# Four transformer layers on one core: the first two batches' keys and values of a 16-head attention are projected in the layer before its own, and VectorE's order in the third layer changes

## The chip, the cores and the metric

The kernel runs on one core of a Trainium2 chip. A core has five engines that run their own instruction streams and meet through semaphores: TensorE (PE in the rows), VectorE (DVE), ScalarE (ACT), GpSimd (POOL) and SyncE (SP), which here only issues DMA transfers. PEld is TensorE's loading of weights, which goes on beside its matrix multiplications. The metric is the device time of one launch in microseconds (us); lower is better.

## The reference

Activations `x` of 8 batches x 256 tokens x 256 features pass four layers, all in float32. Each layer is an attention block and then a feed-forward block, each with a normalization of its input and a residual sum.

- Layer 0: 4-head attention over a context with rotary positions and a mask; then 8 experts (256 to 512 to 256), the best two of each token.
- Layer 1: attention with 16 heads of 16 features. Queries come from the normalized `x`; **keys and values are `ctx @ Wk + bk` and `ctx @ Wv + bv`**, that is, from the context alone, which no layer changes. Then 8 experts again, of which each token takes two.
- Layer 2: an mLSTM block (4 heads, a decay matrix made from gates) and a squared-ReLU block that mixes each token with the one before it.
- Layer 3: attention as in layer 1 with weights of its own; then 8 gated experts with a capacity.

Since the keys and values of layers 1 and 3 depend on `ctx` and weights alone, they can be computed at any time before their attention.

## The kernel before, in words

Each layer with experts is one block of five engine programs: `in_one_block` (line 87) runs on every engine first the attention's program and then the experts'. Between blocks stands a barrier. The order within an engine is the order in which the Python code issues; there is no scheduler. SBUF tensors of a layer are its own, among them `took`, a 1 MB workspace that the attention and the experts share, and `mha_vaug`, which holds the values of two batches beside a column of ones. The weights of all layers (`kept_w_mha` and others) are loaded once at the start.

**16-head attention** (`mha_block`, layers 1 and 3). Batches go through in 64 steps `u` of two heads, eight steps per batch. A step computes scores on TensorE (L560), VectorE reduces each row's extreme (L417, `maximum`), TensorE turns these (L580), VectorE adds them into the queries (L427, `top`), and three steps later TensorE computes the scores again, transposed (L568), ScalarE takes the exponential (L310), and L595 multiplies by the values. `scores(u)` waits for the maxima of step u-1. The next batch is prepared in between, at fixed steps: `turn_x` at step 0, `project_q` at 1, `project_k` at 2 (ScalarE's `keys`, L288, takes it out of PSUM), `project_v` at 4 (VectorE's `values`, L406, at 5). For batch 0 all of it stands in front of the loop. In layer 1 the order there is keys, values, `turn_x` (L499), queries; in layer 3 it is `turn_x`, keys, queries, values. `keep_busy` issues dummy multiplications of a constant (L150). The context of a batch comes by a SyncE DMA into `mha_ctxT` (L233), two slots. At its start ScalarE fills `mha_vaug` with ones (L280).

**Experts** (`moe_block`). Their programs begin with what is left of routing for the last two batches: on TensorE `count(B-2)`, 6 dummy matmuls, `turn(B-1)` (L805), `route(B-1)` (L828), 2 dummies, `count(B-1)`, 6 dummies, a wait for the tile bounds, 18 dummies and then the first tile. VectorE normalizes the last batch (L795), lays out padding rows (`lay_pads`, L1183 to L1192), chooses the experts of the last batch (`choose`, L837 on) and places its tokens; GpSimd then scatters the rows to HBM (L910), and SyncE loads the first tile when all are scattered.

**Third layer** (`l2`). A loop of turns `w_` from 0 to 8: a turn has the mLSTM of batch `w_` and, one turn behind, the feed-forward block of batch `w_-1`. VectorE's part of a turn began with `f_mean_and_var(w_-1)` (L2098 to L2103, on `l_f_stats`), which waits for GpSimd's residual sum (L1967). Then came `weigh` of heads 0 and 1 (L2204: scores in PSUM times the decays that ScalarE made, L2024), `gate_rows` (L2164), `f_normalize` (L2157) and the rest. On TensorE `spread` makes the decays' exponents; `turn_z` (L2373) waits for `gate_rows`, the second `qk` for `weigh` of heads 0 and 1, and `turn_f` (L2350 on `l_fxn`) for `f_normalize`, in this order.

## Time and profile before

| | us |
|---|---|
| median of 3 runs | 1388.36 (1384.16 to 1397.91) |
| profiled execution | 1390.65 |
| its span, first to last instruction | 1388.9 |

| engine | busy us | share of the span |
|---|---|---|
| TensorE | 1263.5 | 91% |
| VectorE | 849.8 | 61% |
| ScalarE | 479.6 | 35% |
| GpSimd | 446.7 | 32% |

The blocks lie on the span as follows: layer 0 from 0 to 322 (its experts from 156), layer 1 from 322 to about 765 (experts from 556), layer 2 to 952, layer 3 to the end. The granted clock of TensorE, mean over the span, is 0.967 of full. In a timeline row stand the start in us, the length, the engine, the line of the code, the operation, what it writes and reads, its count, and in brackets the idle time before it and what ended that.

### The profile page before, as it was taken

What the parts mean: (1) busy time and instruction counts of PE and PEld (TensorE: products, weight loads), DVE (VectorE), ACT (ScalarE), POOL (GpSimd) and SP (SyncE); (2) the same over time, 40 slices, a digit from 0 to 9 for tenths busy, and PEclk for the clock granted to TensorE, in tenths of its full rate; (3) what the DMA queues carried; (4) which work ended last, traced back from release to release, by engine and by line L of the source; (5) the groups of instructions that cost most, each with busy time, mean ns of one, the idle gap of its engine ahead of it and who ended that gap; (6) DMA issues with size and microseconds to landing.
All of it is one profiled execution on the core that took longest, in us unless ns stands there. A gap on an engine that the chain in (4) does not pass through costs nothing. (4 is left out here: it accounts for less than half of the span.)

```text
span 1388.9 us, 31670 instructions
## 1 busy us (share of the span) xinstructions
PE 1263.5 (91%) x9966; PEld 1016.5 (73%) x9966; DVE 849.8 (61%) x2819; ACT 479.6 (35%) x1123; POOL 446.7 (32%) x421
## 2 busy tenths in 40 slices
PE   5899899997899998899999899998899998899995
PEld 4676689995566665799887777876566665799995
DVE  6788444445577876544465588564567776465663
ACT  3655211113456554011111244343556554111110
POOL 1245612222134333522122255432134343222231
PEclk9999899999999999999999998799999999999998
DMA  9201234422101401464654100000001011645523
GB/s 309 71 17 40 93 99 141 134 69 80 46 25 40 165 33 38 138 210 155 200 176 145 51 16 1 1 1 24 8 17 48 33 40 54 212 103 145 146 46 87
DMA packets 87557, 120.08 MB, mean 86 GB/s; under 512 B 11248, under 2 KB 64752, under 8 KB 87152
## 3 DMA queue, kind: packets, MB, share of 16 engines
q1 hardware_dynamic: 48656, 55.20, 12.9%
q10 hardware_dynamic: 25632, 34.85, 7.7%
q0 software_dynamic: 13152, 28.54, 7.3%
q8 instruction: 64, 1.05, 0.3%
q14 instruction: 53, 0.43, 0.1%
HBM read 82.53 MB, written 38.13 MB: 87 GB/s over the span
## 5 line engine op out<-in xcount | busy, mean ns | idle before, releaser
L1351 PEld LDWEIGHTS bank<-f_xT,f_up 128*128 128x128 f32 x2144 | 253.5, 192 | 14.9 <-issue 7.9
L1351 PE MATMUL bank<-f_xT,f_up 128*128 128x128 f32 x2144 | 258.7, 276 | 3.1 <-DVE f_xT L1227 2.1
L417 DVE TENSOR_REDUCE mha_nmax<-bank 128x2 f32<-128x512 f32 x256 | 170.1, 686 | 119.1 <-PE bank L560 95.4
L1360 PE MATMUL bank<-f_down,f_hT 128*128 128x256 f32 x832 | 199.5, 381 | 4.0 <-DVE f_hT L1268 2.8
L310 ACT ACTIVATE l_took<-bank 128x512 f32<-128x512 f32 x256 | 138.9, 598 | 130.8 <-PE bank L568 130.8
L560 PE MATMUL bank<-l_took,mha_q 32*128 32x256 f32 x1024 | 147.7, 406 | 33.2 <-DVE mha_nmax L417 21.8
L1360 PEld LDWEIGHTS bank<-f_down,f_hT 128*128 128x128 f32 x832 | 149.2, 190 | 24.0 <-DVE f_hT L1268 5.6
L1116 POOL DMA_INDIRECT yout<-f_y,f_to x66 | 81.0, 1228 | 244.2 <-DVE f_y L1304 107.6
L568 PE MATMUL bank<-l_took 32*128 32x256 f32 x1024 | 145.5, 406 | 0.7 <-ACT l_took L310 0.7
L560 PEld LDWEIGHTS bank<-l_took,mha_q 32*128 32x128 f32 x1024 | 90.5, 186 | 73.6 <-DVE mha_nmax L417 44.9
L1167 ACT ACTIVATE f_hT<-bank,f_b 128x128 f32<-128x128 f32 x148 | 46.2, 363 | 276.4 <-PE bank L1351 276.4
L150 PE MATMUL bank<-consts 128*128 128x256 f32 x430 | 109.9, 412 | 11.3 <-PEq L69 8.6
L910 POOL DMA_INDIRECT rows<-r_src,r_slots x96 | 95.1, 990 | 59.2 <-DVE r_slots L903 35.1
L150 PEld LDWEIGHTS bank<-consts 128*128 128x128 f32 x430 | 86.5, 207 | 26.2 <-issue 13.6
L1268 DVE TENSOR_SCALAR f_hT<-bank,f_b 128x128 f32<-128x128 f32 x148 | 45.1, 346 | 78.2 <-PE bank L1351 76.4
L568 PEld LDWEIGHTS bank<-l_took 32*128 32x128 f32 x1024 | 87.5, 186 | 2.2 <-issue 2.2
L1162 ACT ACTIVATE f_gate<-bank 128x256 f32<-128x256 f32 x60 | 22.5, 383 | 153.8 <-PE bank L1351 153.8
L260 POOL TENSOR_TENSOR mha_rstd<-mha_var_eps,consts 128x2 f32<-128x2 f32 x16 | 11.6, 726 | 192.9 <-DVE mha_var_eps L386 192.8
L595 PE MATMUL bank<-l_took,mha_vaug 128*32 128x256 f32 x1024 | 70.0, 392 | 1.8 <-ACT l_took L310 1.8
L790 POOL TENSOR_TENSOR r_rstd<-r_var_eps,consts 128x2 f32<-128x2 f32 x24 | 17.7, 737 | 144.3 <-DVE r_var_eps L784 144.3
L595 PEld LDWEIGHTS bank<-l_took,mha_vaug 128*32 128x32 f32 x1024 | 27.1, 110 | 34.8 <-issue 22.1
L1237 DVE COPY f_xt<-l_took 128x256 f32 (+1 forms) x91 | 28.1, 308 | 35.1 <-DMA l_took<-rows 35.0
(290 smaller groups left out, 2278.7 us busy)
## 6 DMA issues: line engine op xcount, KB each, us to landing
l_took<-rows SPq DMA_DIRECT2D x91, 132.0 KB, 2.1
f_up<-in_W ACTq DMA_DIRECT2D x23, 512.0 KB, 4.5
f_down<-in_W ACTq DMA_DIRECT2D x18, 512.0 KB, 5.5
l_took<-rows SPq DMA_DIRECT2D x21, 264.0 KB, 2.8
f_up<-in_W SPq DMA_DIRECT2D x9, 512.0 KB, 7.3
ring<-yout SPq DMA_DIRECT2D x8, 512.0 KB, 4.0
mha_ctxT<-in_ctxT SPq DMA_DIRECT2D x16, 256.0 KB, 2.9
f_down<-in_W SPq DMA_DIRECT2D x6, 512.0 KB, 9.1
```

Of the source, the lines that this page charges most:

```text
L150: pe.matmul(bank[:, 0:S], G.const("ident"), G.consts[:, 0:S], start=True, stop=True)
L310: act.activation(probT[:, n % SLOTS, :, :].rearrange("p c s -> p (c s)"), transposed_in(n)[:, :], ACT.Exp, scale=-1.0).then_inc(prob_ready, 1)
L417: vector.tensor_reduce(nmax[:, p, :, at], ps_s[n % 2][:, :].rearrange("p (k s) -> p k s", s=S), AX.X, ALU.min).then_inc(max_ready, 1)
L560: ins = pe.matmul(ps_s[j][:, part * S:(part + 1) * S], q[row:row + 32, r, p, c, at], k[row:row + 32, r, p, c, :], start=True, stop=True)
L568: ins = pe.matmul(transposed_in(2 * t + j)[:, part * S:(part + 1) * S], k[row:row + 32, r, p, c, at], q_top[row:row + 32, r, p, c, :], sta ...
L595: ins = pe.matmul(values_in(g)[32 * j:32 * j + VW, 0:S], vaug[:, b % 2, c, 4 * i + j, :], probT[:, (4 * g + j) % SLOTS, c, :], start=c == ...
L910: pool.indirect_dma_start(rows[:, :], bass.IndirectOffsetOnAxis(self.slots[:, t, k:k + 1], 0), self.src[:, t, :], None).then_inc(self.scat ...
L1116: pool.indirect_dma_start(away[:, :], bass.IndirectOffsetOnAxis(to[:, k:k + 1], 0), (z if p else y)[:, k, 0:width], None, compute_op=ALU.a ...
L1167: ins = act.activation(hT[:, m, :], ps_h[0][:, m * R:(m + 1) * R], ACT.Relu, bias=b1[:, e, m:m + 1])
L1268: ins = vector.tensor_scalar(hT[:, m, :], ps_h[1][:, (m - 2) * R:(m - 1) * R], b1[:, e, m:m + 1], 0.0, ALU.add, ALU.max)
L1351: ins = pe.matmul(into, up[q][i][:, c, m * P:(m + 1) * P], xT[:, c, :], start=c == 0, stop=c == DC - 1)
L1360: ins = pe.matmul(ps_y[:, 0:D], hT[:, m, :], down[q][:, m, :], start=m == 0, stop=m == HC - 1)
```

## The change

1. A new class `Ahead` projects keys and values of batches 0 and 1 of a 16-head attention in the layer before: those of layer 1 at the start of layer 0's experts, those of layer 3 at the start of layer 1's experts (layer 2 then lies in between and leaves them alone). `took` and `vaug` become tensors of the whole program, so that the results stay.
2. Its context comes by two SyncE DMAs of 256 KB that wait for the last values of the attention (`pv_done`), since they land in its workspace. They stand in SyncE's queue behind the first expert weights and biases, and ahead of the wait for `ends_ready`.
3. Each batch takes 8 matmuls of 128x256 on TensorE, 4 activations on ScalarE and 2 additions on VectorE. The matmuls take the place of the two groups of 6 dummies; the 18 dummies in front of the first tile become 16 in layers 0 and 1; layer 3, which has 24, keeps all of its dummies. TensorE waits for the readers of the new results ahead of the first tile.
4. In `mha_block` nothing of keys and values is left for batches 0 and 1, and the contexts of batches 2 and 3 are loaded at its start. The ones are written once, by GpSimd at the very start of the program.
5. In the third layer VectorE does `weigh` of heads 0 and 1 ahead of `f_mean_and_var`, and `log_forget` ahead of `z_mean_and_var`.

```diff
+            if filled:
+                pool.memset(G.vaug[:, :, :, :, :], 1.0).then_inc(filled, 1)
             attend.gpsimd(pool)
...
+AHEAD = 2
...
+class Ahead:
...
+        self.ctxT = took[:, 6:6 + AHEAD, :, :]
+        self.k = took[:, 12:16, :, :].rearrange("p (r i) c s -> p r i c s", i=2)
+        self.keys_in, self.values_in = (G.PS[6], G.PS[0]), (G.PS[5], G.PS[2])
...
+    def load(self, eng):
+        eng.wait_ge(self.read, self.count)
+        for b in range(AHEAD):
+            eng.dma_start(self.ctxT[:, b, :, :], self.ctx_t[b].rearrange("(c p) n -> p c n", p=P)).then_inc(self.ctx_landed, 16)
+    def project(self, pe, b):
+        if b == 0:
+            pe.wait_ge(self.w_landed, 16 * 2)
+            pe.wait_ge(self.ctx_landed, 16 * AHEAD)
+        for m in range(DC):
+            for c in range(DC):
+                ins = pe.matmul(self.keys_in[b][:, m * S:(m + 1) * S], self.w[:, 1, c, m * P:(m + 1) * P], self.ctxT[:, b, c, :],
+                                start=c == 0, stop=c == DC - 1)
+        ins.then_inc(self.k_done, 1)
+        for i in range(TPB):
+            for c in range(DC):
+                ins = pe.matmul(self.values_in[b][:, i * D:(i + 1) * D], self.ctxT[:, b, c, i * P:(i + 1) * P], self.w[:, 2, c, :],
+                                start=c == 0, stop=c == DC - 1)
+        ins.then_inc(self.v_done, 1)
+    def keys(self, act, b):
+        bk = self.vec[:, 2 * DC:4 * DC]
+        if b == 0:
+            act.wait_ge(self.w_landed, 16 * 2)
+        act.wait_ge(self.k_done, b + 1)
+        for p, rows in enumerate(("even16", "odd16")):
+            for c in range(DC):
+                ins = act.activation(self.k[:, b, p, c, :], self.keys_in[b][:, c * S:(c + 1) * S], ACT.Identity,
+                                     bias=bk[:, DC * p + c:DC * p + c + 1], scale=self.G.const(rows))
+        ins.then_inc(self.k_ready, 1)
+    def values(self, vector, b):
+        bv = self.vec[:, 4 * DC:4 * DC + D]
+        if b == 0:
+            vector.wait_ge(self.w_landed, 16 * 2)
+            if self.filled:
+                vector.wait_ge(self.filled, 1)
+        vector.wait_ge(self.v_done, b + 1)
+        for i in range(TPB):
+            ins = vector.tensor_tensor(self.G.vaug[:, b, i, :, 0:D // MHA_HEADS],
+                                       self.values_in[b][:, i * D:(i + 1) * D].rearrange("p (h v) -> p h v", h=MHA_HEADS),
+                                       bv.rearrange("p (h v) -> p h v", h=MHA_HEADS), ALU.add)
+        ins.then_inc(self.v_ready, 1)
+    def all_read(self, eng):
+        eng.wait_ge(self.k_ready, AHEAD)
+        eng.wait_ge(self.v_ready, AHEAD)
...
-    vaug = sb("vaug", [P, 2, TPB, HEADS, VW])
+    vaug = G.vaug
...
-            after(sync, v_done, b - 1)
-            sync.dma_start(ctxT[:, b % 2, :, :], ctx_t[b].rearrange("(c p) n -> p c n", p=P)).then_inc(ctx_landed[b % 2], 16)
+            if b >= AHEAD:
+                after(sync, v_done, b - 1 - AHEAD)
+                sync.dma_start(ctxT[:, b % 2, :, :], ctx_t[b].rearrange("(c p) n -> p c n", p=P)).then_inc(ctx_landed[b % 2], 16)
...
-        act.activation(vaug[:, :, :, :, :].rearrange("p r i h v -> p (r i h v)"), first(2 * TPB * HEADS * VW), ACT.Identity,
-                       bias=1.0, scale=0.0).then_inc(ones_ready, 1)
         def keys(b):
-            act.wait_ge(k_done, b + 1)
+            if b < AHEAD:
+                act.sem_inc(k_ready, 1)
+                return
+            act.wait_ge(k_done, b + 1 - AHEAD)
...
-            vector.wait_ge(v_done, b + 1)
+            if b < AHEAD:
+                vector.sem_inc(v_ready, 1)
+                return
+            vector.wait_ge(v_done, b + 1 - AHEAD)
...
-            pe.wait_ge(ctx_landed[b % 2], 16 * (b // 2 + 1))
-            after(pe, xnT_ready, b + 1 if b else 0)
-            project(1, ctxT[:, b % 2, :, :], ps_x if b else ps_s[0]).then_inc(k_done, 1)
+            pe.wait_ge(ctx_landed[b % 2], 16 * (b // 2 + 1 - AHEAD // 2))
+            pe.wait_ge(xnT_ready, b + 1)
+            project(1, ctxT[:, b % 2, :, :], ps_x).then_inc(k_done, 1)
...
-        if incoming:
-            project_k(0)
-            project_v(0)
-            turn_x(0)
-            project_q(0)
-        else:
-            turn_x(0)
-            project_k(0)
-            project_q(0)
-            project_v(0)
+        turn_x(0)
+        project_q(0)
...
-            if s == 2 and b + 1 < B:
+            if s == 2 and AHEAD <= b + 1 < B:
...
-            if s == 4 and b + 1 < B:
+            if s == 4 and AHEAD <= b + 1 < B:
...
+        if ahead:
+            ahead.load(sync)
         sync.wait_ge(rt.ends_ready, 1)
...
         rt.turned(act, B - 1)
+        if ahead:
+            ahead.keys(act, 0)
         if BOOST or SUMMED:
             rt.weigh(act, B - 1)
         act.wait_ge(rt.ends_ready, 1)
         rt.pad(act, 0, pads[0], (1,))
+        if ahead:
+            ahead.keys(act, 1)
...
         lay_pads()
+        if ahead:
+            ahead.values(vector, 0)
         rt.choose(vector, B - 1)
         rt.place(vector, B - 1)
         rt.bound(vector)
+        if ahead:
+            ahead.values(vector, 1)
...
         rt.count(pe, B - 2)
-        keep_busy(pe, G, PS[7], 6)
+        if ahead:
+            ahead.project(pe, 0)
+        else:
+            keep_busy(pe, G, PS[7], 6)
         rt.turn(pe, B - 1)
         rt.route(pe, B - 1)
         keep_busy(pe, G, PS[7], 2)
         rt.count(pe, B - 1)
-        keep_busy(pe, G, PS[7], 6)
+        if ahead:
+            ahead.project(pe, 1)
+        else:
+            keep_busy(pe, G, PS[7], 6)
         pe.wait_ge(rt.bounds_ready, 1)
         for p, at in enumerate(passes):
             prime(pe, at.xT_done, at.h_done, at.y_done)
             ends = [end_of(pe, p, 0)]
-            keep_busy(pe, G, PS[7], 28 if p else 24 if GLU else 18)
+            keep_busy(pe, G, PS[7], 28 if p else 24 if GLU else 16)
+            if ahead and p == 0:
+                ahead.all_read(pe)
...
+        sems, took = semaphores(nc, ctx, "l0_"), G.took
         rt = Dispatch(nc, G, ctx, sems, "r0_", "route0", True)
         attend = l0_attention(nc, G, ctx, sems, took, a, rt)
-        experts = moe_block(nc, G, ctx, sems, took, "f0_", rt, (a["W1_0"], a["W2_0"]), (a["b1_0"], a["b2_0"]), leaving=handed)
-        in_one_block(nc, G.PS, rt, attend, experts)
+        ahead = Ahead(G, sems, took, "mha1", a["ctxT"], attend.read, attend.count, sems("vaug_filled"))
+        experts = moe_block(nc, G, ctx, sems, took, "f0_", rt, (a["W1_0"], a["W2_0"]), (a["b1_0"], a["b2_0"]), leaving=handed,
+                            ahead=ahead)
+        in_one_block(nc, G, rt, attend, experts, ahead.filled)
...
+        ahead = Ahead(G, sems, took, "mha3", a["ctxT"], attend.read, attend.count)
...
                 now, more = w_ < B, w_ + 1 < B
-                if w_ >= LAG:
-                    f_mean_and_var(w_ - LAG)
                 if now:
                     weigh(w_, 0)
                     weigh(w_, 1)
+                if w_ >= LAG:
+                    f_mean_and_var(w_ - LAG)
...
+                if more:
+                    log_forget(w_ + 1)
                 if w_ + 3 < B:
                     z_mean_and_var(w_ + 3)
-                if more:
-                    log_forget(w_ + 1)
...
+        took = ctx.enter_context(nc.sbuf_tensor("took", [P, NT, 2, D], F32))
+        vaug = ctx.enter_context(nc.sbuf_tensor("vaug", [P, AHEAD, TPB, MHA_HEADS, MHA_VW], F32))
```

TensorE, start of layer 0's experts, in the kernel before:

```order
L875 MATMUL bank<-r_chosen,r_ones 128x8
L150 MATMUL bank<-consts 128x256 x6
L805 MATMUL bank<-consts,r_src 128x128 x4
L828 MATMUL bank<-kept_w_route,r_xT 128x8 x4
L150 MATMUL bank<-consts 128x256 x2
```

and now:

```order
L941 MATMUL bank<-r_chosen,r_ones 128x8
L193 MATMUL bank<-took,kept_w_mha 128x256 x4
L198 MATMUL bank<-kept_w_mha,took 128x256 x4
L871 MATMUL bank<-consts,r_src 128x128 x4
L894 MATMUL bank<-kept_w_route,r_xT 128x8 x4
L155 MATMUL bank<-consts 128x256 x2
```

Where six dummies stood, the key projection (L193) and the value projection (L198) of batch 0 stand, ahead of the turn of the last batch (L805, now L871).

TensorE, start of layer 1's attention, before:

```order
L150 MATMUL bank<-consts 128x256 x5
L506 MATMUL bank<-mha_ctxT,kept_w_mha 128x256 x4
L534 MATMUL bank<-kept_w_mha,mha_ctxT 128x256 x4
L499 MATMUL bank<-consts,mha_xn 128x128 x4
L506 MATMUL bank<-mha_xnT,kept_w_mha 128x256 x4
L560 MATMUL bank<-l_took,mha_q 128x256 x4
L499 MATMUL bank<-consts,mha_xn 128x128 x4
L560 MATMUL bank<-l_took,mha_q 128x256 x4
L506 MATMUL bank<-mha_xnT,kept_w_mha 128x256 x4
```

and now:

```order
L155 MATMUL bank<-consts 128x256 x5
L575 MATMUL bank<-consts,mha_xn 128x128 x4
L582 MATMUL bank<-mha_xnT,kept_w_mha 128x256 x4
L634 MATMUL bank<-took,mha_q 128x256 x4
L575 MATMUL bank<-consts,mha_xn 128x128 x4
L634 MATMUL bank<-took,mha_q 128x256 x4
L582 MATMUL bank<-mha_xnT,kept_w_mha 128x256 x4
```

The key and value projections of batch 0 (L506 and L534 on `mha_ctxT`) are gone; `turn_x` and the queries follow the dummies.

VectorE, a turn of the third layer, before:

```order
L2121 SCALAR_TENSOR_TENSOR X<-l_fused,l_z_rstd,X 128x256 x2
L2098 BN_STATS l_f_stats<-X 128x6 x2
L2101 BN_AGGR l_f_moments<-l_f_stats 128x2 x2
L2103 TENSOR_SCALAR l_f_var_eps<-l_f_moments 128x2
L2204 SCALAR_TENSOR_TENSOR l_cT<-bank,l_decay 128x384 x2
L2164 TENSOR_SCALAR l_z_rows<-bank,kept_gate_bias 8x256
L2157 TENSOR_SCALAR l_fxn<-X,l_f_moments,l_f_rstd 128x256 x2
```

and now:

```order
L2201 SCALAR_TENSOR_TENSOR X<-l_fused,l_z_rstd,X 128x256 x2
L2284 SCALAR_TENSOR_TENSOR l_cT<-bank,l_decay 128x384 x2
L2178 BN_STATS l_f_stats<-X 128x6 x2
L2181 BN_AGGR l_f_moments<-l_f_stats 128x2 x2
L2183 TENSOR_SCALAR l_f_var_eps<-l_f_moments 128x2
L2244 TENSOR_SCALAR l_z_rows<-bank,kept_gate_bias 8x256
L2237 TENSOR_SCALAR l_fxn<-X,l_f_moments,l_f_rstd 128x256 x2
```

`weigh` of two heads (L2204, now L2284) has moved from behind the feed-forward block's moments to ahead of them; `gate_rows` (now L2244) follows the moments.

## Rows read from the trace of the kernel before

**Rows 1.** The page: busy time by engine; two DMA issues (KB each, us to landing)

```profile
PE 1263.5 (91%) x9966; PEld 1016.5 (73%) x9966; DVE 849.8 (61%) x2819; ACT 479.6 (35%) x1123; POOL 446.7 (32%) x421
...
mha_ctxT<-in_ctxT SPq DMA_DIRECT2D x16, 256.0 KB, 2.9
...
f_down<-in_W SPq DMA_DIRECT2D x6, 512.0 KB, 9.1
```

**Rows 2.** Timeline (start, us, engine, line), layer 1's first heads

```profile
332.58 0.76 DVE L406 TENSOR_TENSOR mha_vaug<-bank,kept_v_mha 128x256 f32<-128x256 f32 x2
...
333.25 0.99 DVE L448 TENSOR_SCALAR mha_q<-bank,mha_q_scale,mha_nbq 128x256 f32<-128x256 f32 x2
...
334.34 1.13 PE L560 MATMUL bank<-l_took,mha_q 32*128 32x256 f32 x8 [1.72 <-ACT mha_q L303]
...
335.95 0.66 PE L499 MATMUL bank<-consts,mha_xn 128*128 128x128 f32 x4 [0.48 <-POOL mha_xn L246]
```

**Rows 3.** Timeline, layer 1, values of batch 1

```profile
350.04 2.60 PE L534 MATMUL bank<-kept_w_mha,mha_ctxT 128*128 128x256 f32 x8
...
350.62 0.68 DVE L417 TENSOR_REDUCE mha_nmax<-bank 128x2 f32<-128x512 f32 x1
...
352.57 0.48 PE L560 MATMUL bank<-l_took,mha_q 32*128 32x256 f32 x2
```

**Rows 4.** Timeline, fourth layer's attention, its start

```profile
956.77 1.89 PE L506 MATMUL bank<-mha_ctxT,kept_w_mha 128*128 128x256 f32 x8
...
962.05 1.13 PE L560 MATMUL bank<-l_took,mha_q 32*128 32x256 f32 x8
...
965.62 3.58 PE L506 MATMUL bank<-mha_xnT,kept_w_mha 128*128 128x256 f32 x8
...
972.45 1.93 ACT L288 ACTIVATE l_took<-bank,kept_v_mha,consts 128x256 f32<-128x256 f32 x4 [1.28 <-PE bank L506]
```

**Rows 5.** Timeline, from layer 0's attention to its experts, TensorE

```profile
148.29 1.08 PE L1781 MATMUL bank<-l_took,a_v 128*64 128x256 f32 x8
...
156.31 4.52 PE L150 MATMUL bank<-consts 128*128 128x256 f32 x12
...
161.96 0.66 PE L805 MATMUL bank<-consts,r_src 128*128 128x128 f32 x4 [1.13 <-DVE r_src L795]
```

**Rows 6.** Timeline, layer 1's experts, routing of the last batch

```profile
562.58 0.18 DVE L837 TENSOR_TENSOR r_logits<-bank,kept_b_route 128x16 f32<-128x16 f32 x1 [0.19 <-PE bank L828]
```

**Rows 7.** Timeline, third layer, VectorE's first turn, then one later turn

```profile
778.41 0.87 DVE L2121 SCALAR_TENSOR_TENSOR X<-l_fused,l_z_rstd,X 128x256 f32<-128x256 f32 x2
...
836.86 1.89 DVE L2121 SCALAR_TENSOR_TENSOR X<-l_fused,l_z_rstd,X 128x256 f32<-128x256 f32 x2
...
837.54 1.35 ACT L2024 ACTIVATE l_decay<-bank,l_g 128x256 f32<-128x256 f32 x4 [1.18 <-PE bank L2409]
...
838.54 1.33 POOL L1967 TENSOR_TENSOR X<-X,l_h 128x512 f32<-128x512 f32 x1
...
839.91 0.75 DVE L2098 BATCH_NORM_STATS2 l_f_stats<-X 128x6 f32<-128x256 f32 x2 [1.16 <-POOL X L1967]
...
841.10 1.02 DVE L2204 SCALAR_TENSOR_TENSOR l_cT<-bank,l_decay 128x384 f32<-128x384 f32 x2
...
841.23 0.71 POOL L1954 TENSOR_TENSOR l_f_rstd<-l_f_var_eps,consts 128x2 f32<-128x2 f32 x1
...
842.43 0.71 DVE L2157 TENSOR_SCALAR l_fxn<-X,l_f_moments,l_f_rstd 128x256 f32<-128x256 f32 x2
...
842.55 0.29 PE L2373 MATMUL bank<-consts,l_z_rows 8*128 8x8 f32 x2 [0.89 <-DVE l_z_rows L2164]
...
844.18 1.11 PE L2350 MATMUL bank<-consts,l_fxn 128*128 128x128 f32 x4
```

**Rows 8.** Windows, third layer, TensorE: length, busy (count), granted clock, DMA share, GB/s

```profile
863.00:879.00 16.00, 16.00 (x66) 0.57 0.01 2
...
887.00:899.00 12.00, 12.00 (x56) 0.57 0.01 2
```

49 lines of the change are left out of this document (27 added, 22 removed).

## The prediction

> **What bounds the kernel now.** I read the page first, then a timeline of each place that the change touches, then windows for TensorE's clock. The page shows TensorE busy for 1263.5 us of the span [rows 1]: what stands in its queue is nearly always on the path, but only where it is not waiting for someone. So I ask at each place what TensorE waits for. In a 16-head attention the loop is a round trip of TensorE and VectorE: scores, maxima, scores. A projection put between two steps is free as long as it fits beside VectorE's maxima, and costs only the rest. Where the routing of the last batch runs, in front of the experts, TensorE waits for VectorE and dummies fill its time. In the third layer the path runs through VectorE and GpSimd and back to TensorE, and TensorE stands idle in front of L2373 [rows 7].
>
> The sum is made against the profiled execution, 1390.65 us, which is 2.3 above the median of 1388.36. What a measurement tells from no change is about 1%, 13.9 us: 1374.5 and 1402.2 are the bounds.
>
> **Part 1: keys and values leave the start of the attention.**
>
> *Layer 1, batch 0.* The first scores start at 334.34 [rows 2]. In front of them VectorE adds the values from 332.58 for 0.76 and scales the queries from 333.25 for 0.99. Without the additions the queries come 0.67 earlier, and so would the first scores, to 333.7. But `turn_x` of batch 1 stands next on TensorE and waits for GpSimd's `mha_xn` until 335.95, which the change does not touch [rows 2]; only the scores behind it can profit. I take 0.2, between 0 and 0.7.
>
> *Layer 1, batch 1.* Of its keys, the 4 activations (1.93 by the row of layer 3 [rows 4]) stood ahead of the first exponentials, which step 4 waits for; without them I take 0.4. Of its values, TensorE's projection takes 2.60 from 350.04, and the next scores start at 352.57, while VectorE's last maximum is done at 350.62 + 0.68 = 351.30 [rows 3]. A handover from VectorE to TensorE takes at least 0.1 (334.24 to 334.34 [rows 2]); the scores could start at 351.4 or some tenths later: 0.9. The key projection in step 2 lay beside VectorE's maxima: 0. Layer 1 in all: **-1.5**.
>
> *Layer 3, batch 0.* Here the keys (1.89 from 956.77) stand between `turn_x` and the queries, which need only ScalarE's copy of the turned input; that copy can run beside the keys, so between 0 and 1.89 of them is uncovered, and I take half, 0.9. The first scores (962.05) and all behind come 0.9 earlier [rows 4]. Batch 1 as in layer 1: 0.3 for the exponentials behind 1.93 us of ScalarE at 972.45, 1.0 for the values. Layer 3: **-2.2**.
>
> The bounds of both together: 0 if something else is late each time; and 16 us if all the TensorE time counted, four projections per layer at 1.89 [rows 4] to 2.60 [rows 3]. I stay near the low end, because the waits decide. Steps 2 and 5 and the ones (now GpSimd's, at the start of the program, where GpSimd has nothing to do) cost nothing: their cover is VectorE's maxima and the first loads.
>
> **Part 2: they arrive in front of the experts.**
>
> *Layer 0.* The last values of the attention end at 148.29 + 1.08 = 149.37; SyncE then issues two loads of 256 KB, which land in a median of 2.9 [rows 1], by about 153. TensorE wants them at 156.31 [rows 5]: 3 us to spare. Instead of 12 records of dummies (4.52 us, mostly at half clock) it runs 16: 4 more, 0.9 us at full clock or 1.7 at half. The dummies ended at 160.83, and the turn of the last batch started at 161.96 [rows 5]. So the delay is 0 to 0.6; **+0.3**. VectorE's additions (0.76 [rows 2]) fit in its wait for the logits. The second batch's projection replaces 6 + 2 dummies out of 24: TensorE's work ahead of the first tile stays 24 matmuls.
>
> *Layer 1.* The four extra records are covered there too, but not VectorE's additions: VectorE was idle only 0.19 ahead of the logits of the last batch [rows 6], since it lays out twice the padding. 0.76 less 0.19 goes on the path to the last scatter and so to the first tile: **+0.5**. What ScalarE gets (twice 1.93 per layer) it does while it waits. On its queue the padding DMAs of later experts are behind it, which nobody needs for some us.
>
> SyncE's queue: behind the wait for `pv_done` stand the padding row and the first tiles, which wait for `ends_ready` much later anyway.
>
> **Part 3: VectorE's order in the third layer.** In the turn shown, VectorE finished L2121 at 838.75 and stood idle for 1.16 until GpSimd's sum ended (838.54 + 1.33 = 839.87). ScalarE had the decays of heads 0 and 1 ready at 837.54 + 1.35 = 838.89 [rows 7]. The two `weigh`s need 1.02: from 838.9 to 839.9, into the hole. The moments still run from 839.91 to 841.1, but `gate_rows` follows at once instead of behind `weigh` (841.10 + 1.02 = 842.1), so that L2373 on TensorE starts near 841.7 instead of 842.55: 0.85. `f_normalize` waits for GpSimd's root, 841.23 + 0.71 = 841.94, and starts near 842.0 instead of 842.43. L2350, which comes behind `qk`, then goes from 844.18 to about 843.4: **-0.8 per turn**, handed on through ScalarE's copy and the mixing to the next turn. That holds for turns 1 to 5. Turns 6 and 7 have no L2121, so their waits are shorter: 0.3 and 0.2. In all **-4.5**, between 0 and -6.5. `log_forget` moves within a run of VectorE work of the same length: 0.
>
> Here a shared port is what could spoil it. L2121 takes 0.87 beside an idle GpSimd and 1.89 beside a busy one [rows 7], and the moved `weigh`s would now run beside GpSimd's L1967. The Trainium skill (GPSIMD Engine Reference, Key points) says that GpSimd shares its SBUF interfaces with VectorE and that contention is with instructions in a two-port mode or with two SBUF inputs. L2121 has two SBUF inputs; `weigh` has one and one in PSUM, so by that rule it stays at 1.02 and the -4.5 stands; the other outcome is rival D.
>
> **Clock.** In the third layer TensorE ran at a granted 0.57 for 16 us and again for 12 us [rows 8], which is mostly 1.2 instead of 2.4 GHz. At full clock the same work is 9.1 and 6.8 us: 12 us lost. Both stretches come right behind a wait of the kind that Part 3 shortens (0.89 idle ahead of L2373 [rows 7] in a neighbouring turn). If the waits shrink, some falls may not come. I take **-3**, a quarter, between +14 (two falls more) and -12.
>
> Sum: -1.5 - 2.2 + 0.3 + 0.5 - 4.5 - 3 = -10.4, so 1380.2 beside 1390.65; the runs' median lies 2.3 below the profiled execution, of which I give half to chance, and forecast **1379**, 1.2 below the sum; so do the rivals. Its own range is 1375 to 1385.
>
> **Rivals.**
>
> A. *The third layer keeps its clock.* All of the falls go, 9 us of the 12 lost instead of 3 (some is hidden behind VectorE): 1373. For it: the falls follow waits. Against it: not every such wait was followed by one, and idle remains.
>
> B. *The attention starts run at half clock.* Between the dummies and the first scores TensorE now has only a turn and a query projection, with waits between. The query projection of batch 1 already took 3.58 at 965.62 [rows 4], against 1.89 for one at full clock. If that of batch 0 and some scores join it, 1.7 to 2 each per layer, the 3.7 of Part 1 are gone: 1383. The Trainium skill (TensorE: Matmul & The Clock Gate, "What's actually happening") says that the slow clock is the default and activity releases it, which speaks against a change that takes matmuls away at a start.
>
> C. *More falls in the third layer, slower than before.* The place is the same, the sign the other: its busy pattern shifts and two more of the eight turns fall as that at 863 did, each losing 16 x 0.43 = 6.9 [rows 8]. Sum without the clock term -7.4, plus 13.8: 1396. From the second extra fall on the change is a loss. Against it: TensorE gets denser there, not emptier.
>
> D. *`weigh` collides with GpSimd.* It grows by 1.89/0.87 to 2.2, the moments start 1.2 late, and a turn loses 0.4 instead of gaining 0.8: over five turns +2 instead of -4.5, and no clock gain. 1390.65 - 2.9 + 2 - 1.2 = 1389.
>
> E. *The context comes late.* If the loads took 9.1 as the slowest kind on that queue [rows 1], they would land at 159.4, the turn of the last batch would slip to 159.4 + 6.8 at half clock = 166.2, 4.3 later than 161.96, and layer 1 would lose 2.5: 1386.
>
> **Chances.** The forecast 0.52, A 0.18, B 0.12, C 0.06, D 0.06, E 0.06. The range goes from A's lower side to above D: **1369 to 1391**; left out are C and the far tail of A. Faster by over 1% needs below 1374.5: most of A and the lower tail of the forecast, 0.21. Slower by over 1% is only the far end of C, 0.02. Within 1%: 0.77.
>
> **What would show it.** Part 1: the first scores of layer 3 some 0.9 earlier counted from the block's start, of layer 1 hardly; the ends of both attentions' first 8 steps 1.5 to 2.5 earlier. Part 2: the turn of the last batch in layer 0 within 0.6 of where it was, and in layer 1 the logits' addition 0.5 later. Part 3: no `weigh` between the moments and `gate_rows`, `weigh` at 1.02, idle ahead of L2373's counterpart under 0.2, and a turn at full clock 0.8 shorter. The clock: windows of the third layer with less than 28 us near 0.57. I am wrong if the attention starts show longer idle or half-clock projections, if `project` waits for its context, or if the third layer gets no shorter.

## The result, and the profile after

| | before | changed |
|---|---|---|
| median, us (18 runs each) | 1387.71 (1374.66 to 1397.91) | 1376.65 (1373.39 to 1383.0) |
| profiled execution; its span | 1390.65; 1388.9 | 1376.92; 1375.2 |
| granted clock, mean over the span | 0.967 | 0.968 |

The ratio is 0.9924 with a 95% interval of 0.9905 to 0.9942: 11 us faster at the median, within the 1% that I had called no change. The forecast was 1379, the range 1369 to 1391. The number is close, but two of its terms are not: the attentions gained nothing, and the third layer gained more than twice what I gave it.

The engines' busy times on the page of the changed kernel answer to [rows 1]. TensorE has 56 records fewer and 18 us less busy time. The records themselves weigh some 13 us at full clock (an estimate: 8 of this kind take 1.89 [rows 4]). The rest is a sum of opposite signs: in the third layer's loop alone TensorE is busy 14.5 us less with the same work (the windows in experiment 4), and at the attention starts the same work takes longer than before, as the next rows show. The attentions' own context loads are 12 instead of 16 and land as fast as before.

```profile
PE 1245.4 (91%) x9910; PEld 999.7 (73%) x9910; DVE 851.0 (62%) x2819; ACT 476.6 (35%) x1121; POOL 448.3 (33%) x422
...
mha_ctxT<-in_ctxT SPq DMA_DIRECT2D x12, 256.0 KB, 3.0
```

**Where the time went**, by the same instruction in both profiled executions (changed minus before, us). To the start of layer 1: -0.6. Layer 1's attention to its last values: +0.6. To the logits of its last batch: +0.4; to the end of its experts: -0.1. To the first moments of the third layer's feed-forward: +2.4. The seven turns from there to the last moments: **-16.8** (135.9 to 119.1). Layer 3's attention with its start: +0.4; the rest nothing. The sum is -13.7.

**The start of layer 1**, TensorE's timeline of the changed kernel (start, us, engine, line; in brackets the idle time before and what ended it), beside [rows 2]:

```profile
327.77 1.12 PE L575 MATMUL bank<-consts,mha_xn 128*128 128x128 f32 x4 [3.65 <-DVE mha_xn L319]
329.56 3.78 PE L582 MATMUL bank<-mha_xnT,kept_w_mha 128*128 128x256 f32 x8 [0.68 <-ACT mha_xnT L369]
334.47 2.08 PE L634 MATMUL bank<-took,mha_q 32*128 32x256 f32 x8 [1.14 <-ACT mha_q L377]
...
337.90 2.08 PE L634 MATMUL bank<-took,mha_q 32*128 32x256 f32 x8 [0.30 <-DVE mha_nmax L493]
339.91 3.78 PE L582 MATMUL bank<-mha_xnT,kept_w_mha 128*128 128x256 f32 x8
```

The projections of keys and values had filled TensorE's wait for `mha_xn`. Now it stands idle for 3.65 us, and then the query projection (L582) takes 3.78 us; the one at full clock in the kernel before took half of that. The same scores (L634) take 2.08 where [rows 2] have 1.13. The next fence gives windows of the same execution: length, busy (count) of each engine, then the granted clock (0.50 is 1.2 GHz), DMA share, GB/s.

```profile
328.00:336.00 8.00, 6.19 (x20) 4.26 (x19) 4.56 (x11) 1.61 (x3) 5.25 (x5) 0.50 0.24 80
336.00:344.00 8.00, 7.70 (x26) 4.80 (x24) 3.37 (x6) 0.86 (x2) 0.38 (x1) 0.50 0.00 0
```

The same two windows of the kernel before:

```profile
328.00:336.00 8.00, 5.13 (x29) 3.73 (x27) 6.62 (x16) 3.36 (x7) 4.53 (x5) 1.00 0.33 98
336.00:344.00 8.00, 7.79 (x36) 5.62 (x37) 4.23 (x9) 2.52 (x5) 1.25 (x1) 0.79 0.00 0
```

By the granted clock TensorE was at its lower level for all 16 us, behind the 3.65 us in which it did nothing. The Trainium skill (TensorE: Matmul & The Clock Gate, "What's actually happening") calls the slow clock the default and activity what releases it; this trace agrees.

**A turn of the third layer** in the changed kernel, beside [rows 7]:

```profile
820.63 1.36 ACT L2104 ACTIVATE l_decay<-bank,l_g 128x256 f32<-128x256 f32 x4 [1.18 <-PE bank L2489]
...
821.64 1.33 POOL L2047 TENSOR_TENSOR X<-X,l_h 128x512 f32<-128x512 f32 x1
...
821.76 1.01 DVE L2284 SCALAR_TENSOR_TENSOR l_cT<-bank,l_decay 128x384 f32<-128x384 f32 x2
...
823.00 0.75 DVE L2178 BATCH_NORM_STATS2 l_f_stats<-X 128x6 f32<-128x256 f32 x2 [0.23 <-POOL X L2047]
...
824.15 0.47 DVE L2244 TENSOR_SCALAR l_z_rows<-bank,kept_gate_bias 8x256 f32<-8x256 f32 x1
...
824.68 0.28 PE L2453 MATMUL bank<-consts,l_z_rows 8*128 8x8 f32 x2
...
824.89 0.92 PE L2501 MATMUL bank<-l_xnT,l_ctxT 64*128 64x256 f32 x8
825.06 0.73 DVE L2237 TENSOR_SCALAR l_fxn<-X,l_f_moments,l_f_rstd 128x256 f32<-128x256 f32 x2 [0.44 <-POOL l_f_rstd L2034]
...
825.85 0.66 PE L2430 MATMUL bank<-consts,l_fxn 128*128 128x128 f32 x4
```

`weigh` (L2284) sits in the hole that VectorE had ahead of the moments (1.16 us, now 0.23), takes 1.01 us with GpSimd's sum (L2047) running beside it, and `turn_z` (L2453) follows without the 0.89 us of idle time. From the moments to the turn of `l_fxn` it is 2.85 us where [rows 7] have 4.27. Not all of these 1.42 us are the order's: in the turn of [rows 7] the clock fell just behind `turn_z`, and the second `qk` (L2421, now L2501) took 1.48 where it now takes 0.92. Its row, and two windows of the kernel before around it:

```profile
842.77 1.48 PE L2421 MATMUL bank<-l_xnT,l_ctxT 64*128 64x256 f32 x8
...
842.00:843.00 1.00, 0.45 (x4) 0.43 (x6) 1.00 (x4) 1.00 (x5) 0.00 (x0) 0.99 0.00 0
843.00:846.00 3.00, 3.00 (x17) 2.62 (x16) 1.46 (x6) 0.83 (x4) 0.00 (x0) 0.50 0.00 0
```

One wait remains in each turn of the new order: 0.73 us ahead of the mixing (L2539), where the old order had about 0.9 ahead of `turn_z` and 0.5 at another place:

```profile
814.45 0.92 PE L2539 MATMUL bank<-l_w,l_mixed 128*128 128x256 f32 x3 [0.73 <-DVE l_mixed L2326]
```

The lengths of the seven turns, from moments to moments (the starts of L2098 and L2178 on `l_f_stats`):

| profile | turns, us | sum |
|---|---|---|
| before | 18.87, 18.63, 19.64, 24.18, 22.13, 17.23, 15.25 | 135.9 |
| changed | 17.89, 17.76, 17.76, 17.76, 16.43, 16.51, 15.00 | 119.1 |

### The profile page after: what moved, and what is told of

Its sections match the earlier page's. It is cut to its first block and busy times, and to the rows that moved or that the text cites. A ratio compares the mean times of both kernels' runs of the same rounds, so it can differ in the third digit from the quotient of the medians.

```text
span 1375.2 us, 31569 instructions
## 1 busy us (share of the span) xinstructions
PE 1245.4 (91%) x9910; PEld 999.7 (73%) x9910; DVE 851.0 (62%) x2819; ACT 476.6 (35%) x1121; POOL 448.3 (33%) x422
## 5 line engine op out<-in xcount | busy, mean ns | idle before, releaser
L634 PE MATMUL bank<-took,mha_q 32*128 32x256 f32 x1024 | 152.6, 416 | 38.3 <-DVE mha_nmax L493 30.5
L384 ACT ACTIVATE took<-bank 128x512 f32<-128x512 f32 x256 | 139.0, 598 | 134.6 <-PE bank L642 134.6
L634 PEld LDWEIGHTS bank<-took,mha_q 32*128 32x128 f32 x1024 | 93.4, 193 | 80.7 <-DVE mha_nmax L493 50.4
L642 PE MATMUL bank<-took 32*128 32x256 f32 x1024 | 147.0, 409 | 0.7 <-ACT took L384 0.7
L155 PE MATMUL bank<-consts 128*128 128x256 f32 x374 | 91.6, 399 | 10.9 <-PEq L69 8.4
L642 PEld LDWEIGHTS bank<-took 32*128 32x128 f32 x1024 | 88.4, 188 | 2.2 <-issue 2.2
L155 PEld LDWEIGHTS bank<-consts 128*128 128x128 f32 x374 | 72.4, 199 | 23.0 <-issue 13.2
L669 PE MATMUL bank<-took,vaug 128*32 128x256 f32 x1024 | 70.2, 393 | 1.8 <-ACT took L384 1.8
L669 PEld LDWEIGHTS bank<-took,vaug 128*32 128x32 f32 x1024 | 27.1, 110 | 34.8 <-issue 22.1
L1303 DVE COPY f_xT<-bank 128x256 f32<-128x256 f32 x108 | 44.9, 416 | 5.0 <-PE bank L1418 4.7
```

Source lines behind the costliest of these rows:

```text
L155: pe.matmul(bank[:, 0:S], G.const("ident"), G.consts[:, 0:S], start=True, stop=True)
L384: act.activation(probT[:, n % SLOTS, :, :].rearrange("p c s -> p (c s)"), transposed_in(n)[:, :], ACT.Exp, scale=-1.0).then_inc(prob_ready, 1)
L634: ins = pe.matmul(ps_s[j][:, part * S:(part + 1) * S], q[row:row + 32, r, p, c, at], k[row:row + 32, r, p, c, :], start=True, stop=True)
L642: ins = pe.matmul(transposed_in(2 * t + j)[:, part * S:(part + 1) * S], k[row:row + 32, r, p, c, at], q_top[row:row + 32, r, p, c, :], sta ...
L669: ins = pe.matmul(values_in(g)[32 * j:32 * j + VW, 0:S], vaug[:, b % 2, c, 4 * i + j, :], probT[:, (4 * g + j) % SLOTS, c, :], start=c == ...
```

## The experiments

Theory: the gain is all in the third layer, part of it shorter turns and part a clock that no longer falls; the attentions gained what I said and lost it again because their starts run at half clock. (A fall is a stretch in which the granted clock is 0.50.) Rivals: the third layer's clock was luck of one profile; the half clock hides behind VectorE; the projection ahead is worth nothing in any case.

"Step n" below is the start of the n-th pair of heads' scores, in us from the attention's first ScalarE instruction (on `mha_nbq`), each from one profile. The places of dummies and projections ("behind step 2") go by the loop's own count `u`, which begins with 0. "Kernel n" is that of experiment n. Ratios are to the kernel before on the same chip.

**1. VectorE's order alone**, in the kernel before:

```diff
+                if now:
+                    weigh(w_, 0)
+                    weigh(w_, 1)
                 if w_ >= LAG:
                     f_mean_and_var(w_ - LAG)
-                if now:
-                    weigh(w_, 0)
-                    weigh(w_, 1)
...
+                if more:
+                    log_forget(w_ + 1)
                 if w_ + 3 < B:
                     z_mean_and_var(w_ + 3)
-                if more:
-                    log_forget(w_ + 1)
```

> The kernel before with only VectorE's new order in the third layer (both swaps), keys and values untouched. Theory (all of the change's gain is made in the third layer, by 1.0 us a turn at full clock and by the clock falls that no longer come): the third layer's loop, 135.9 us from the first to the last moments before, comes down to about 119 as in the changed kernel, and the time is 0.99 of before, 1374 to 1378 us, as good as the whole change. Rival (the two parts need each other, or the clock of the third layer was luck of the profiled run): only 5 to 6 us are gained, 0.996, and falls to half clock still stand in the loop. Prediction as on record: 1380.2 - (-1.5 - 2.2 + 0.3 + 0.5), so 0.9945 of before.

Measured: 1373.89 (10 runs), ratio 0.9913 (0.9884 to 0.9942). Turns 18.13, 17.75, 17.76, 17.74, 16.42, 16.53, 14.98. The whole gain of the change comes from moving a few VectorE instructions; the two intervals overlap, so that this version is no worse is all that they tell.

**2. The projection ahead alone**: the changed kernel with that order undone.

> The changed kernel with VectorE's two swaps in the third layer undone, so that only the projection ahead is left. Theory (the attentions gain nothing, since their starts now run at half clock): within 0.3% of before, 1384 to 1392, the first turns of the third layer at 18.9 us again and falls to half clock at some of the turns. Rival (the projection ahead gains its 2.9 us as on record and the trace of the changed kernel had bad luck): 0.998, with the first scores of layer 3 at 0.9 less from the block's start and its eighth step 2 us less.

Measured: 1389.38 (12 runs), ratio 1.0015 (0.9989 to 1.0041). Turns 18.63, 18.62, 18.75, 18.63, 18.95, 17.23, 15.25. Layer 1's first scores stand at 12.49 and its step 14 at 58.91 (before: 12.17 and 55.76). So the larger part of the change, taken alone, gains nothing.

**3. Dummies in the place of the wait** that the order shortens, in the kernel before:

```diff
                 if more:
+                    fill(w_, 2)
                     turn_z(w_ + 1)
```

> The kernel before with two dummy matmuls (four records, 0.9 us) ahead of each turn_z in the third layer, where TensorE waited 0.9 us for VectorE; VectorE's order is the old one. Theory (the falls to half clock come from that wait): no stretch of the third layer under 0.9 in turns 1 to 5, the turns all near 18.9 us, 11 to 12 us gained less 0.1 to 0.3 a turn for dummies that end late: 1377 to 1380, 0.993. Rival (the falls have another cause, such as the wait at another place or chance): falls remain, the time stays within 0.3% of before or rises by up to 7 us for seven turns in which the dummies stand in the way.

Measured: 1384.93 (12 runs), ratio 0.9973 (0.9945 to 1.0001). The profile has a granted clock of 1.00 over the loop and turns of 19.48, 18.62, 18.73, 18.74, 17.35, 17.85, 15.24, that is 126.0, of which about 1.6 is dummies in the way. The median came down by less than I expected, 3.4 us, and its interval touches no change. The direction fits the theory, but the runs alone do not show it. The profiled execution, which has no fall in the loop, took 1384.57 and so lies at the median: the small gain does not need falls in the other runs. Its loop is 9.9 us shorter than in the first profile of before, but only 3.4 shorter than in the second (experiment 4), which has fewer falls.

**4. Is the fall a matter of luck?** The kernel before and kernel 2 were each profiled once more.

> The kernel before once more, for a second look at the clock of its third layer. Theory (falls to half clock in its loop are common but not the same in every execution, and make its times scatter): some turns of the third layer longer than 18.7 us again, at other places than in the first profile, the loop between 125 and 136 us from the first moments to the last. Rival (the falls belong to the order of the work): the same turns 3, 4 and 5 at 19.6, 24.2 and 22.1 us.

> The projection ahead without VectorE's new order once more, whose first profile was of its fastest execution and had hardly a fall in the third layer. Theory (falls common, of changing place): the loop between 125 and 136 us again, most likely longer than the 126.1 of the first look. Rival (with the projection ahead the third layer keeps its clock): 124.5 to 126.2 us.

Measured, single runs: 1390.2 and 1389.06, with 1379.86 for one more run of before beside them. Turns of before: 18.87, 18.61, 19.73, 22.48, 17.23, 17.23, 15.25; of kernel 2: 18.62, 18.62, 22.45, 18.62, 22.14, 17.23, 15.25. The windows over the loop, TensorE's busy time first, the granted clock third from the end. Kernel before, first profile:

```profile
802.00:938.00 136.00, 129.70 (x846) 105.49 (x845) 97.52 (x300) 62.28 (x132) 63.03 (x53) 0.90 0.02 5
```

Kernel before, second profile:

```profile
809.00:938.00 129.00, 122.70 (x844) 99.94 (x843) 97.54 (x300) 62.24 (x132) 62.67 (x52) 0.95 0.01 4
```

Kernel 2 (projection ahead, old order), second profile:

```profile
805.00:937.00 132.00, 125.44 (x842) 102.25 (x841) 96.74 (x299) 62.27 (x132) 62.81 (x52) 0.92 0.02 5
```

The changed kernel:

```profile
805.00:924.00 119.00, 115.25 (x845) 94.04 (x844) 97.62 (x299) 62.19 (x132) 62.65 (x53) 1.00 0.02 6
```

Kernel 1 (new order alone):

```profile
801.00:920.00 119.00, 115.13 (x845) 93.68 (x843) 97.33 (x299) 62.13 (x132) 62.95 (x53) 1.00 0.02 6
```

VectorE's busy time is the same within 1% in all five; only TensorE's changes, with its clock. In the old order all four profiles have falls (loops of 135.9, 129.4, 132.9, 126.1), in turns 3 to 5 but not always the same; in the new order the loop is 119.1 to 119.4 in each of its nine profiles. Put together from turns without a fall, the old order's loop is 18.87 + 18.61 + 18.62 + 18.62 + 17.23 + 17.23 + 15.25 = 124.4. So the order gives 5.1 us of work (124.4 to kernel 1's 119.3), and the clock gave another 1.7 to 11.5, by the execution; the kernel before's first profile, which the prediction read, had lost the most.

What comes right ahead of a fall can be read too. In the four profiles of the old order TensorE waits sixteen times for 0.7 us or more ahead of `turn_z` in the loop. Eight of these waits are followed by a fall, which begins 0.2 to 1.3 us behind the start of `turn_z`, and the loop has no other fall; in the kernel before's first profile these are the waits of 0.89, 0.88 and 0.70 at 842.55, 862.20 and 886.37, while that of 1.13 at 823.92 is followed by none.

**5. Dummies at the attention starts**, in the changed kernel:

```diff
         keep_busy(pe, G, ps_t[0], 5)
+        if incoming:
+            keep_busy(pe, G, ps_o, 7)
         turn_x(0)
+        keep_busy(pe, G, ps_o, 1)
         project_q(0)
+        keep_busy(pe, G, ps_o, 2)
...
             if s == 1 and b + 1 < B:
                 project_q(b + 1)
+            if u in (0, 2):
+                keep_busy(pe, G, ps_o, 2 if u else 1)
```

> The changed kernel with dummy matmuls at both 16-head attention starts where the projections had been: in layer 1 seven ahead of turn_x(0), in both layers one behind it, two behind the queries, one behind step 0 and two behind step 2. Theory (what the attentions gained was lost again to half clock): the query projection of batch 0 in layer 1 takes 2.0 instead of 3.8, the first scores 1.1 instead of 2.1, layer 1's first eight steps end 2 to 3 us earlier than in the changed kernel and layer 3's 1 to 3, in all 3 to 5 us or 0.997 of the changed kernel, 1371 to 1374. Rival (half clock hides behind VectorE's round trip): the clock is full but no step starts earlier, or the dummies come in the way: within 1 us of the changed kernel.

Measured: 1368.32 (6 runs), ratio 0.9874 (0.9837 to 0.9911). TensorE's timeline of this kernel in layer 1:

```profile
327.60 0.60 PE L575 MATMUL bank<-consts,mha_xn 128*128 128x128 f32 x4
...
328.88 1.99 PE L582 MATMUL bank<-mha_xnT,kept_w_mha 128*128 128x256 f32 x8 [0.24 <-ACT mha_xnT L369]
...
332.06 1.13 PE L634 MATMUL bank<-took,mha_q 32*128 32x256 f32 x8 [0.32 <-ACT mha_q L377]
```

1.99 for 3.78 and 1.13 for 2.08: the prices at full clock again. They hold only as far as the next wait: behind 1.10 us for `mha_xn` of batch 1 the second scores take 2.08 again:

```profile
334.29 1.12 PE L575 MATMUL bank<-consts,mha_xn 128*128 128x128 f32 x4 [1.10 <-POOL mha_xn L319]
...
336.19 2.08 PE L634 MATMUL bank<-took,mha_q 32*128 32x256 f32 x8
```

Ten dummies in layer 1 and three in layer 3 ahead of the first scores, and three behind, bring step 14 from 57.59 to 53.60 in layer 1 and from 52.66 to 49.00 in layer 3. The median moved by 8 (7 by the ratios), more than the 3 to 5 expected; 3.2 of it in the profiles is the third layer's start, which no edit of this kernel touches.

**6. Which of them count.** Once with only those ahead of the first scores, once with only those between the steps:

> The changed kernel with only those dummies that stand ahead of the first scores of both 16-head attentions (seven ahead of turn_x(0) in layer 1, one behind it, two behind the queries). Theory (the start of the attention decides the clock): in layer 1 the first scores come 1.4 us earlier from the block's start than in the changed kernel (11.3 to 11.4), in layer 3 nothing changes there (8.6 to 9.5); without dummies in step 2 the step after it still waits 1.3 to 1.4 us, and the clock may fall there. About half of the eight us that all dummies brought: 1371 to 1374. Rival (only the clock between the steps matters): 1375 to 1377, as the changed kernel.

> The changed kernel with only the dummies behind step 0 and behind step 2 of the first batch, the place from which the key projection of batch 1 was taken away. Theory (that projection, counted at nothing because it lay beside VectorE's maxima, kept the clock up for the steps behind it): layer 3's steps 3 to 6 come 2 to 3 us earlier from the first scores than in the changed kernel, layer 1's start stays as in the changed kernel (first scores at 12.8 from the block's start), in all 1371 to 1374. Rival (the start alone decides): as the changed kernel, 1375 to 1377.

Measured: 1370.40 (6 runs), ratio 0.9896 (0.9847 to 0.9945), and 1372.98 (12 runs), 0.9912 (0.9876 to 0.9948); the two intervals overlap, so the times do not tell them apart. The profiles do by place, in us from the attention's start:

| | layer 1: step 1, 6, 13 | layer 3: step 1, 6, 14 |
|---|---|---|
| before | 12.17, 30.40, 52.59 | 9.61, 27.87, 52.35 |
| changed | 12.92, 30.79, 54.42 | 8.66, 26.62, 52.66 |
| ahead of scores only | 11.52, 28.75, 52.53 | 9.60, 26.82, 52.38 |
| between steps only | 12.78, 30.93, 54.51 | 7.68, 24.34, 49.74 |
| both (kernel 5) | 11.43, 29.12, 50.42 | 9.60, 23.39, 49.00 |

In layer 1 the dummies between the steps are worthless alone. Layer 3 needs care, since its first scores differ by the execution: the same attention code, without dummies, has them at 8.66, 7.68, 9.60 and 8.39 in four profiles (the changed kernel, the two of kernel 2, kernel 8). So the way from step 1 to step 6 tells more: 18.0 in the changed kernel, 17.2 with the dummies ahead of the scores, 16.7 with those between the steps, 13.8 with both. So the dummies between the steps, those behind step 2 in the place of the key projection that I had counted at nothing, help there, and most together with those ahead of the scores. One profile each stands behind this.

**7. All of it, and more dummies**: those of 5 (in layer 1 two ahead of `turn_x(1)` in place of the one behind it), two more behind steps 3 and 4, and

```diff
-        if ahead:
-            ahead.values(vector, 0)
         rt.choose(vector, B - 1)
+        if ahead:
+            ahead.values(vector, 0)
...
             centre(2)
+            keep_busy(pe, G, ps_s[0], 5)
             sum_up(0)
```

> The changed kernel with dummies at all of these places, two more behind steps 3 and 4, in layer 1 two ahead of turn_x(1) in place of the one behind it, five ahead of the first sum_up in the third layer (where TensorE waited 2.65 us for VectorE), and VectorE's first additions of values behind choose instead of ahead of it. Theory: layer 1 loses no 0.4 us at the logits of the last batch; the third layer's start goes from 60.5 to 57 us or less, with full clock behind sum_up; the steps of layer 3 keep full clock. 1 to 4 us below the version with dummies at the starts alone: 1364 to 1367. Rival (each filled wait costs what it gives): 1367 to 1370.

Measured: 1365.60 (6 runs), ratio 0.9852 (0.9805 to 0.9899). VectorE's timeline at the logits of the last batch in layer 1, the changed kernel first:

```profile
562.29 0.74 DVE L221 TENSOR_TENSOR vaug<-bank,kept_v_mha 128x256 f32<-128x256 f32 x2
562.95 0.17 DVE L903 TENSOR_TENSOR r_logits<-bank,kept_b_route 128x16 f32<-128x16 f32 x1
```

and this kernel:

```profile
557.64 0.17 DVE L913 TENSOR_TENSOR r_logits<-bank,kept_b_route 128x16 f32<-128x16 f32 x1 [0.19 <-PE bank L904]
...
559.13 0.75 DVE L221 TENSOR_TENSOR vaug<-bank,kept_v_mha 128x256 f32<-128x256 f32 x2
559.80 0.18 DVE L957 TENSOR_TENSOR r_rank<-bank,r_running 128x32 f32<-128x32 f32 x1
```

The wait of 0.19 is that of [rows 6] again, and the logits are 14.86 us behind the last values, as before, instead of 15.25. Of these 0.4 us the first tile gets only 0.2 (31.22 behind the last values, 31.44 in the changed kernel): the additions now fill most of VectorE's wait for the ranks, and these start right behind them. The third layer's start (from the end of layer 1's expert tiles to the first moments) was 2.4 us longer than before in the changed kernel and is 1.7 shorter here.

**8. `log_forget` put back** behind `z_mean_and_var`, in the changed kernel:

> The changed kernel with one of VectorE's two swaps undone: log_forget stands behind z_mean_and_var again. Prediction as on record: nothing, 1375 to 1378, turns of 17.76 us. Rival (log_forget is on the way to the next turn's decays and its place gives part of the gain of a turn): turns of 17.9 to 18.6, 1378 to 1382.

Measured: 1376.94 (12 runs), ratio 0.9945 (0.9913 to 0.9976). Turns 17.90, 17.77, 17.90, 17.77, 16.41, 16.53, 14.98. This swap is worth nothing; `weigh` is all of it.

**9. The control: dummies, and nothing projected ahead.** Kernel 1 with:

```diff
             turn_x(0)
+            keep_busy(pe, G, ps_t[0], 1)
             project_q(0)
+            keep_busy(pe, G, ps_t[0], 3)
         else:
...
+            if u == 0 and incoming:
+                keep_busy(pe, G, ps_t[0], 2)
             if s == 0 and b + 1 < B:
                 turn_x(b + 1)
+            if u == 0 and not incoming:
+                keep_busy(pe, G, ps_t[0], 1)
...
+            if u == 3:
+                pe.wait_ge(v_ready, 1)
+                keep_busy(pe, G, ps_o, 3)
...
             centre(2)
+            keep_busy(pe, G, ps_s[0], 5)
             sum_up(0)
```

> The control to the last dummies: nothing is projected ahead (the attention of the kernel before, VectorE's new order in the third layer), but dummies fill TensorE's waits in the attention starts: one behind turn_x(0) and three behind the queries in layer 1, two ahead of turn_x(1) in layer 1 and one behind it in layer 3, three behind step 3 in both, and five ahead of the first sum_up in the third layer. Theory (with the clock held up in both, the projection ahead is worth what its prediction said and somewhat more): the clock is full in both attention starts, layer 1's fourteenth step starts at 53.5 from the block's start against 50.0 with projection ahead and dummies, layer 3's at 49.5 against 45.9, so this kernel lies 6 to 8 us above that one: 1371 to 1374. Rival (the dummies alone are the gain, the projection ahead is worth nothing even then): within 2 us of that one, 1364 to 1368.

> The version with dummies at all places once more, beside the control on one chip: 1363 to 1367 as in its first run. If it lies over 1368, the first comparison was luck.

Measured, side by side: 1366.38 (6 runs), ratio 0.9836 (0.9799 to 0.9872), and 1362.55 (6 runs), 0.9808 (0.9770 to 0.9845). The difference of the medians is 3.8 us, under the 6 to 8 of the theory and over the 2 of the rival; the control's 1366.38 itself lies in the range of the rival (1364 to 1368). The intervals against the kernel before overlap, but both ran on one chip, and of the 36 pairs of one run of each, the one with the projection ahead is the faster in 34. The two kernels also differ in where their dummies stand. The step times are sharper:

| us from the attention's start | steps 1 to 6 | step 14 |
|---|---|---|
| layer 1, dummies only | 11.91, 14.47, 17.46, 20.62, 23.78, 26.95 | 51.44 |
| layer 1, ahead and dummies | 11.36, 14.18, 17.17, 20.01, 22.59, 25.43 | 50.06 |
| layer 3, dummies only | 8.82, 11.32, 14.31, 17.47, 20.63, 23.81 | 49.21 |
| layer 3, ahead and dummies | 7.68, 10.16, 13.14, 16.05, 18.63, 21.47 | 45.95 |

This is what Part 1 is worth when both kernels keep their clock at the starts; to the last values of the attention 1.2 us of it are left in layer 1 and 1.9 in layer 3. The fastest version of the study, at 0.981 of the kernel before, is the one with all dummies:

```profile
324.00:356.00 32.00, 27.14 (x212) 18.66 (x210) 22.34 (x56) 9.77 (x20) 10.95 (x10) 1.00 0.20 67
928.00:960.00 32.00, 26.19 (x218) 17.40 (x218) 18.38 (x46) 12.25 (x27) 10.82 (x10) 1.00 0.06 18
```

Its first 32 us of both attentions have a granted clock of 1.00; the changed kernel's:

```profile
322.00:354.00 32.00, 22.14 (x110) 14.54 (x108) 18.75 (x48) 6.90 (x13) 6.60 (x6) 0.69 0.19 68
938.00:970.00 32.00, 24.82 (x142) 15.81 (x142) 14.26 (x38) 8.78 (x19) 7.79 (x8) 0.68 0.06 17
```

## Why the prediction came out near the number, step by step

| term | predicted | changed kernel | with the clock held (experiment 9) |
|---|---|---|---|
| Part 1, layer 1 | -1.5 | +0.6 | -1.4 at step 14, -1.2 at the last values |
| Part 1, layer 3 | -2.2 | +0.3 at step 14, +0.4 at the last values | -2.3 at step 6, -3.3 at step 14, -1.9 at the last values |
| Part 2, layer 0 | +0.3 | 0.0 | |
| Part 2, layer 1 | +0.5 | +0.4 at the logits, +0.6 at the first tile | |
| Part 3, order | -4.5 | -5.1 | |
| clock, third layer's loop | -3 | -11.5, by the profiled pair | |
| third layer's start | not in the sum | +2.4 | |

- **Part 1: the mechanism was right, the net result wrong.** Its waits are there. With the clock held, layer 1's first scores gain 0.55 (I had said 0 to 0.7 and taken 0.2), the step behind the exponentials 0.6 (20.01 and 22.59 beside 20.62 and 23.78; said 0.4) and that behind the values 0.3 (said 0.9, from a 2.60 us projection of [rows 3], which takes 1.89 in the control: I had priced it at a fallen clock). In layer 3 the queries gain 1.14 (said 0.9) and batch 1's work 1.2 to step 6 (said 1.3). The step that failed is "cost nothing: their cover is VectorE's maxima": the key projection of step 2 delays the next step by 0.3 (from the third to the fourth entry of the table 3.16 with it and 2.84 without), and above all it kept TensorE's clock up for the steps behind it, and so did the projections in front of the first scores. Rival B, given 0.12, is what happened, with its own price: 1.8 us on the query projection of batch 0 and 0.95 on the scores in layer 1; in layer 3 from step 2 on. Longer idle (3.65 us) and half-clock projections at an attention start are also the first of the three signs of being wrong that the prediction named.
- **Part 2: right.** `project` had no wait for its context. The turn of layer 0's last batch came 0.26 earlier, but so did the last values ahead of it (0.25), so the projection cost nothing there. VectorE's additions put 0.40 on layer 1's logits. Rival E is out.
- **Part 3: right, a little small.** -0.74, -0.86, -0.86, -0.88, -0.81, -0.70 and -0.27 by turn, against five times -0.8, -0.3 and -0.2; turn 6 was mis-sized. `weigh` stayed at 1.01 beside GpSimd, so rival D is out.
- **Clock of the loop: the size was off.** I took a quarter of the 12 us that [rows 8] show as lost; it was all of it, as in rival A (0.18), whose 1373 the median missed because Part 1 gave nothing and the third layer's start took longer. The 11.5 is also the most of four profiles (11.5, 8.5, 5.0, 1.7), so that the pair of profiles overstates what a usual run gained. That it follows the order and not chance is shown by four profiles against nine. That the wait ahead of `turn_z` is what brings the falls is likely: all eight come right behind it, and experiment 3, which fills it in the old order, has none in its one profile. But only half of these waits bring one, the 0.73 us ahead of L2539 in the new order bring none, and the runs of experiment 3 gained just 3.4 us with an interval that touches no change. How much waiting a turn bears is not shown.
- **What I had no term for**: the third layer's start. TensorE waits 2.65 us there for `l_lf` in both kernels, and behind it the clock is down for longer in the changed one. It is so in the second profile of before too, whose start is only 0.3 longer than in the first, so this explains the +2.4 in part at most. The seven profiles with the projection ahead and no dummies there have -0.8 to +2.5, the four without it -0.4 to +0.6: it may be the execution, the change, or both, and this stays open. With five dummies in that wait the start is shorter than before in all three profiles that have them (-1.7, -2.1, -2.1).

So the total came out within 3 us in part by luck: the mechanisms of Parts 2 and 3 held, but the 4.5 us that Part 1 failed to give and the 2.4 at the third layer's start happened to be paid by 8.5 more from the clock. The tiles of layer 1's experts differ by 4.1 us between the two profiles of the kernel before, and by -0.3 to +2.8 in the other kernels; I did not find out why, and no conclusion rests on them.

## What to carry to other kernels

Work on TensorE that nobody waits for may still pay for the clock of what comes behind it: when it is moved away, put dummies of the same length in the hole, or measure the move with and without them. Look for idle time of a second engine just ahead of an instruction that it must wait for, and move into it whatever is ready: nine tenths of a microsecond a turn here, and a loop whose clock no longer fell. When a change has two parts, time each alone: here the small one was worth 14 us and the large one nothing until its holes were filled, and 4 us then.

## What the runs showed of the hardware

- One and the same query projection of 8 records takes 1.99 us or 3.78, and 8 records of scores 1.13 or 2.08, by the granted clock (2.4 or 1.2 GHz, 1.00 or 0.50 in the windows).
- Idle time ahead of a fall can be small: behind eight of sixteen waits of 0.7 to 1.1 us ahead of `turn_z`, in turns of 17 to 19 us, the clock fell to half as in [rows 8], in changing turns of the same program. Without that wait no fall came in the loop in ten profiles (nine of the new order, and experiment 3), though the new order keeps a wait of 0.73 us at another place.
- On VectorE the two instructions of `weigh`, with one source in PSUM, take 1.01 us beside a busy GpSimd and 1.02 beside an idle one. The two of L2121, with both sources in SBUF, grow from 0.87 to 1.89 [rows 7], and it is the second alone that grows, to 1.49: the first takes 0.48 although GpSimd works beside most of it.
- The scatter of a kernel's runs goes with the clock: of the 27 runs of before beside experiment 1, the five fastest have a mean granted clock of 0.973 to 0.978 and the five slowest 0.958 to 0.971. From fastest to slowest it is 23 us in 18 runs of before, 10 in as many of the changed kernel, 7 in the 6 runs of experiment 9 with dummies at all places.
